# VectorE's list reordered around the copies of the maxima, and the transposed x evacuated by ScalarE, in a windowed-attention layer

## The reference

```python
def _arsinh_norm(x, w, b):
    return w * jnp.arcsinh(x) + b
...
nb_k = kk[:, ri, ci].reshape(B, H, W, k * k, num_heads, hd)
nb_v = v[:, ri, ci].reshape(B, H, W, k * k, num_heads, hd)
scores = jnp.einsum('bijnd,bijmnd->bijnm', q, nb_k)
attn = jax.nn.softmax(scores, axis=-1)
out = jnp.einsum('bijnm,bijmnd->bijnd', attn, nb_v).reshape(B, H, W, C)
return out @ proj_w + proj_b
...
h1 = _arsinh_norm(h, n1_w, n1_b)
h = h + _na2d(h1, qkv_w, qkv_b, proj_w, proj_b)
h2 = _arsinh_norm(h, n2_w, n2_b)
ff = jax.nn.gelu(h2 @ mlp_w1 + mlp_b1, approximate=False) @ mlp_w2 + mlp_b2
return h + ff
```

## Time and profile before

| | |
|---|---|
| median of three runs | 4443.3 us |
| the profiled execution's own time | 4440.94 us |
| its span | 4439.1 us |
| mean granted TensorE clock (share of full speed) | 0.992 |
| TensorE matmul busy | 4159.5 us, 94% |
| VectorE busy | 3926.1 us, 88% |
| ScalarE busy | 3631.7 us, 82% |
| GpSimd busy | 3359.0 us, 76% |

### The profile page before, as it was taken

The page is one execution under the profiler, slowest core; times in us unless marked ns, Lnnn a source line. Parts: engine busy times, 40 slices in busy tenths (PEclk is TensorE's granted clock), DMA queues, the critical chain, the costliest instruction groups (busy, mean ns, idle before and its releaser), DMA issues.

```text
span 4439.1 us, 129514 instructions
## 1 busy us (share of the span) xinstructions
PE 4159.5 (94%) x49224; PEld 2857.8 (64%) x49224; DVE 3926.1 (88%) x8225; ACT 3631.7 (82%) x5377; POOL 3359.0 (76%) x4092
## 2 busy tenths in 40 slices
PE   5999999999999999999999999999999999999997
PEld 3666666666666666666666666666666666666664
DVE  6899999989989998998999899899989989999984
ACT  4888888888888888888888888888888888888884
POOL 2777777777777777777777777777777777777775
PEclk8999999999999999999999999999999999999998
DMA  4555555555555555555555555555555555555551
GB/s 120 132 141 139 142 139 143 136 139 141 141 140 140 142 137 139 141 140 141 140 142 137 140 141 139 140 141 141 139 139 144 136 140 140 141 141 138 142 133 50
DMA packets 644105, 607.94 MB, mean 137 GB/s; under 512 B 77070, under 2 KB 639376, under 8 KB 639888
## 3 DMA queue, kind: packets, MB, share of 16 engines
q1 hardware_dynamic: 643488, 599.66, 51.2%
HBM read 206.02 MB, written 135.40 MB: 77 GB/s over the span
## 4 chain that ended last, share of the span: by engine, by line
DVE 42%; PE 18%; POOL 13%; issue 13%; ACT 12%; SPq 1%; DMA 0%; POOLq 0%; DVEq 0%; ACTq 0%
PE ps L381 16%; POOL b_lo L1163 6%; POOL b_hi L1161 6%; DVE ps L841 5%; DVE queries L860 5%; DVE o_norm L874 4%; DVE ln_u L767 4%; DVE ln_u L760 4%; DVE k_nat L815 4%; ACT L1073 4%; DVE ln_u L763 3%; DVE h L802 3%; ACT p_hi L1064 3%; DVE q_nat L808 3%; ACT prob L1063 2%
## 5 line engine op out<-in xcount | busy, mean ns | idle before, releaser
L1146 POOL TENSOR_TENSOR p_lo<-prob,p_hi 100x512 f16<-100x512 f32 x1024 | 1269.7, 1245 | 619.1 <-ACT p_hi L1064 619.1
L1063 ACT ACTIVATE prob<-ps 100x512 f32<-100x512 f32 x1024 | 610.2, 596 | 51.1 <-PE ps L381 49.3
L874 DVE TENSOR_TENSOR o_norm<-ps,recip 64x128 f32<-64x128 f32 x2048 | 590.2, 288 | 49.3
L1172 POOL TENSOR_TENSOR g_lo<-g,g_hi 128x512 f16<-128x512 f32 x512 | 593.8, 1160 | 41.0
L1064 ACT ACTIVATE p_hi<-ps 100x512 f16<-100x512 f32 x1024 | 616.4, 602 | 0.0
L381 PEld LDWEIGHTS ps<-v_win,p_hi 100*128 100x128 f16 x8192 | 476.0, 98 | 204.7 <-issue 66.9
L381 PE MATMUL ps<-w_hi,g_hi 128*128 128x256 f16 x2048 | 561.1, 274 | 0.0
L841 DVE TENSOR_REDUCE ps<-ps 128x8 f32<-128x800 f32 x512 | 509.1, 994 | 58.6 <-PE ps L381 54.2
L381 PE MATMUL ps<-w_lo,g_hi 128*128 128x256 f16 x2048 | 560.9, 274 | 0.0
L381 PE MATMUL ps<-w_hi,g_lo 128*128 128x256 f16 x2048 | 560.8, 274 | 0.0
L381 PE MATMUL ps<-v_win,p_hi 100*128 100x65 f16 x8192 | 515.6, 193 | 27.0 <-POOL p_lo L1146 18.4
(11 more groups left out here) (100 smaller groups left out, 11497.9 us busy)
## 6 DMA issues: line engine op xcount, KB each, us to landing
keys<-k_win SPq DMA_DIRECT2D x1536, 100.0 KB, 2.3
v_win<-v_rows SPq DMA_DIRECT2D x1024, 101.6 KB
queries<-q_nat SPq DMA_DIRECT2D x1536, 64.0 KB
v_rows<-v_nat SPq DMA_DIRECT2D x256, 260.0 KB, 4.3
xin<-in_x_dram SPq DMA_DIRECT2D x128, 512.0 KB, 4.3
out_dram<-y SPq DMA_DIRECT2D x256, 256.0 KB, 3.0
queries<-in_query_mask_dram SPq DMA_DIRECT2D x128, 224.0 KB
keys<-in_mlp_w_dram SPq DMA_DIRECT2D x2, 512.0 KB, 6.5
```

The costliest lines, as they stand in the source:

```text
L874: s = v.tensor_tensor(o_norm[r, c], av[r, :, HD * e:HD * e + HD], recip[c % 2][r].to_broadcast([NQ, PAIRS, HD]), ALU.mult)
L1063: act.activation(prob[b][0:NK], ps[0:NK, B_ST + b, :], ACT.Exp, scale=INV * INV).then_inc(prob_ready, 1)
L1146: pool.tensor_tensor(p_lo[b][0:NK], prob[b][0:NK], p_hi[b][0:NK], ALU.subtract).then_inc(p_lo_ready, 1)
L1172: pool.tensor_tensor(g_lo[:, m, :], g32[:, m, :], g_hi[:, m, :], ALU.subtract).then_inc(g_lo_ready, 1)
```

## The change

Three things. (1) On VectorE, in slots 2 and 3 the instructions `sign2`, `sign1` and `o_low` 0 come ahead of `maximum`, `maximum_high` and `maximum_low` instead of behind them, with `sign1` now ahead of `o_low`; in slots 0, 1 and 2 the instructions `k_low` 1, `q_low` 1 and `sum1` come ahead of the two copies `maxima_to_queries` instead of behind. (2) `x_from_transposes` leaves VectorE for ScalarE, as an activation Copy with a scale; there it stands around `v_high` 0 in slot 1, behind `root2`. (3) On TensorE, `max_rows` of slot 3 goes behind `mlp_in` 2.

```diff
@@ -195,7 +195,8 @@
             sem("pe_" + s) for s in ("x", "q", "k", "v", "proj", "m1", "m2"))
         pe_s, pe_max, pe_st, pe_av, pe_ot = (sem("pe_" + s) for s in ("s", "max", "st", "av", "ot"))
 
-        xT_ready, h_ready, abs1, abs2, sum1, sum2 = (sem("dve_" + s) for s in ("xT", "h", "abs1", "abs2", "sum1", "sum2"))
+        h_ready, abs1, abs2, sum1, sum2 = (sem("dve_" + s) for s in ("h", "abs1", "abs2", "sum1", "sum2"))
+        xT_ready = sem("act_xT")
         asinh1, asinh2, y_ready = (sem("dve_" + s) for s in ("asinh1", "asinh2", "y"))
         q_lo_ready, k_lo_ready, v_lo_ready, o_lo_ready = (sem("dve_" + s) for s in ("q_lo", "k_lo", "v_lo", "o_lo"))
         max32_ready, max_hi_ready, max_ready, maxima_placed = (
@@ -668,7 +669,7 @@
 
                     if att:
                         weighted(t, par, 2 * k)
-                    if more:
+                    if k < 3 and more:
                         max_rows(ahead[0], ahead[2])
 
                     if k == 0 and post:
@@ -688,6 +689,9 @@
                         turn(t, 0)
                     if k == 3 and post:
                         mlp_in(t - 1, 2)
+                    if k == 3 and more:
+                        max_rows(ahead[0], ahead[2])
+                    if k == 3 and post:
                         mlp_in(t - 1, 3)
 
                     if att:
@@ -751,11 +755,6 @@
                 assert count[0] == V_ALL, count[0]
                 v.memset(keys[:, :, HEADS * TILES * NK:KROW], 0.0).then_inc(keys_zeroed, 1)
 
-            def x_from_transposes(t, u, g):
-
-                v.wait_ge(pe_x, signals(t, G, g + 1))
-                v.tensor_scalar(xT[u][:, g, :], ps[:, X_BANK[g], :], WS, None, ALU.mult).then_inc(xT_ready, 1)
-
             def magnitude(out, of, s):
                 v.tensor_single_scalar(out.bitcast(U32), of.bitcast(U32), MAGNITUDE, ALU.bitwise_and).then_inc(s, 1)
 
@@ -877,8 +876,6 @@
 
             def opening(t):
 
-                x_from_transposes(t + 3, t + 3, 0)
-                x_from_transposes(t + 3, t + 3, 1)
                 if t == -3:
                     magnitude1(0, 0)
                     for t_ in k_win:
@@ -912,6 +909,12 @@
                 for k in range(SLOTS):
                     ta, ka = (t, k + 1) if k + 1 < SLOTS else (t + 1, 0)
                     more = has(ta)
+                    if k == 2 and post:
+                        sign2(t - 1, old)
+                    if k == 3 and fill:
+                        sign1(t + 3, (u + 3) % XT)
+                    if k == 3 and att:
+                        o_low(t, par, 0)
                     if more:
                         maximum(ta, ka)
                         maximum_high(ta, ka)
@@ -923,35 +926,26 @@
                         k_low(t + 2, 0)
                     if k == 1 and pre:
                         q_low(t + 2, par, 0)
-                    if k == 2 and post:
-                        sign2(t - 1, old)
-                    if k == 3 and att:
-                        o_low(t, par, 0)
-                    if k == 3 and fill:
-                        sign1(t + 3, (u + 3) % XT)
 
                     if att:
                         sum_reciprocal(t, 2 * k)
                         normalise(t, 2 * k)
+                    if k == 0 and pre:
+                        k_low(t + 2, 1)
+                    if k == 1 and pre:
+                        q_low(t + 2, par, 1)
+                    if k == 2 and fill:
+                        sum1_(t + 3)
                     if more:
                         maxima_to_queries(ta, par if ta == t else old, ka)
 
-                    if k == 0 and pre:
-                        k_low(t + 2, 1)
                     if k == 0 and post:
                         h_from_projection(t - 1, old, (u - 1) % XT, 0)
                         h_from_projection(t - 1, old, (u - 1) % XT, 1)
-                    if k == 1 and pre:
-                        q_low(t + 2, par, 1)
-                    if k == 1 and fill:
-                        x_from_transposes(t + 3, (u + 3) % XT, 0)
-                        x_from_transposes(t + 3, (u + 3) % XT, 1)
                     if k == 1 and post:
                         sum2_(t - 1)
                     if k == 1 and pre:
                         v_low(t + 2, 0)
-                    if k == 2 and fill:
-                        sum1_(t + 3)
                     if k == 2 and fin:
                         result(t - 2, 0)
 
@@ -992,6 +986,11 @@
 
                 act.wait_ge(ln, signals(t, 1, 1))
                 act.activation(s, s, ACT.Exp, scale=0.5).then_inc(rt, 1)
+
+            def x_from_transposes(t, u, g):
+
+                act.wait_ge(pe_x, signals(t, G, g + 1))
+                act.activation(xT[u][:, g, :], ps[:, X_BANK[g], :], ACT.Copy, scale=WS).then_inc(xT_ready, 1)
 
             def square1(t, u):
                 act.wait_ge(xT_ready, signals(t, G, G))
@@ -1074,6 +1073,8 @@
 
             def opening(t):
 
+                x_from_transposes(t + 3, t + 3, 0)
+                x_from_transposes(t + 3, t + 3, 1)
                 square1(t + 3, t + 3)
                 log_of_square(ln1_s[:], sq1, ln1a, t + 3)
                 root(ln1_s[:], ln1a, root1, t + 3)
@@ -1121,8 +1122,13 @@
                     if k == 1 and post:
                         log_of_square(ln2_s[:], sq2, ln2a, t - 1)
                         root(ln2_s[:], ln2a, root2, t - 1)
+                    if k == 1 and fill:
+                        x_from_transposes(t + 3, (u + 3) % XT, 0)
                     if k == 1 and pre:
                         v_high(t + 2, 0)
+                    if k == 1 and fill:
+                        x_from_transposes(t + 3, (u + 3) % XT, 1)
+                    if k == 1 and pre:
                         v_high(t + 2, 1)
                     if k == 2 and fill:
                         square1(t + 3, (u + 3) % XT)
```

## The result

The changed kernel takes 4766.8 us (4764.67 to 4766.91), the kernel before beside it 4442.4: ratio 1.0729 [1.0708, 1.0750]. Forecast were 4521 and a range that ended at 4540. The sign was right; the loss is 324 us in place of 78. A fourth run of the changed kernel took 5836.72 us at a mean granted clock of 0.656, and is left out as a slow run. The profiled execution takes 4766.82 us, its span is 4765.0.

What follows compares the result with a forecast made beforehand. A ring through all engines, 33.74 us a band, was taken as the bound. Both collisions add 0.63 a band: 123 x 0.63 = 77.5 on 4440.9 gives 4518, with 2.4 to the median 4521; range 4388 to 4540.

Steps and rivals of the forecast that it cites:

- the forecast's case: Slot 0: `magnitude2` stands behind one GpSimd `p_low`, held 0.76 in the replay; band 34.37 with all other steps.
- Ring and span: A ring through all engines sets the 33.74 us band; 0.63 lost per band, times 123, ends left at 0.
- Slot 0, the timing: `k_low` 1 ahead of the copies: `p_low` 2 starts at 13.8, `magnitude2` arrives at 14.01, in its middle.
- Slot 0, the price: Hold of `magnitude2` behind `p_low` 2, bounds 0 and 0.8; 0.8 taken, 0.76 in the replay.
- Slot 1: `q_low` 1 ahead of the copies, x copied by ScalarE: second `x_transposes` 19.10, before 19.25; `v_product` 1 19.69, before 19.84.
- just hidden: Slot 1: ScalarE's copy of x, 18.61 to 19.2, fits behind the transposes (0.59), so `v_product` 1 doesn't wait.
- rival (d): ScalarE, 1.2 us a band fuller, becomes the bound before `v_product` 1: 0 to 0.4 a band; no separate chance given.
- Slot 2: `maximum` waits behind `sign2`, so TensorE's `max_rows` comes 0.62 later; with `mlp_in` 0's wait given back, net 0.28 late.
- Slot 3: `p_low` 6 is first by 0.08, holds `sign1` for 1.0; `mlp_in` 2 starts at 35.10 against 34.43.
- (a): One of two collisions doesn't happen: band 33.99 (about 4474) if `magnitude` isn't held, 34.12 (4490) if `sign1` is first; chance 0.20.
- (c): VectorE never stands behind GpSimd, the four `sum` and `sign` at 1.22 each: band 33.29, 4388; chance 0.27.
- the replay: One band followed from the table load at 4.34 to the next, keeping measured spacings: 38.71 against 38.08.

Runs made afterwards that it cites:

- e2: Changed kernel with one wait added: GpSimd starts `p_low` 2 only after `magnitude2`; 4478.5 us, 1.0084 of the kernel before.
- e6: Changed kernel with one wait added between `p_low` 2 and 3: GpSimd starts `p_low` 3 only after `magnitude2`; 4551.6 us, 1.0253 of the kernel before.
- e3: Kernel before with one edit alone: `k_low` 1 ahead of the copies of the maxima in slot 0; 4550.1 us, 1.0251.
- e7: e2 with three repeats of `magnitude2`'s own operation ahead of it on VectorE, about 1.75 us of plain work intended; 4807.8 us, 1.0832 of the kernel before.
- e1: Changed kernel with one edit undone: `k_low` 1 behind the copies of the maxima again in slot 0; 4571.5 us, 1.0293 of the kernel before.
- e10: e6 with one more wait: GpSimd starts `p_low` 6 only after `sign1`; 4567.4 us, 1.0279 of the kernel before.
- e4: Kernel before with one edit alone: x's two copies out of PSUM on ScalarE, around `v_high` 0; 4455.3 us, 1.0032.
- e8: Kernel before with `q_low` 1 ahead of the copies, x on ScalarE (first copy ahead of `root2`), and last `g_lo` waiting for `sum2`; 4433.5 us, 0.9988.
- e5: Kernel before with only `sign2`, `sign1`, `o_low` 0 ahead of the maxima in slots 2 and 3, and `max_rows` behind `mlp_in` 2; 4586.9 us, 1.0334.

## Why the prediction was right or wrong

The band, step by step of measured kernels, from 33.73:

| | band, us | what is added |
|---|---|---|
| e2 | 34.02 | all edits, `magnitude2` not held |
| e6 | 34.63 | `magnitude2` held by one `p_low` (the forecast's case, 34.37) |
| changed, clock up | 35.60 | held by two |
| changed, clock falls | 36.79 | TensorE at 1.2 GHz behind the stall |

- **Ring and span: right.** The loss is in the band alone, times 123, and a hold of VectorE goes into the band about one for one: a hold of 0.63 costs 0.76 in e3, and 0.61 from e2 to e6.
- **Slot 0, the timing: right.** `k_low` 1 early, ScalarE's windows early, `p_low` 2 ahead of `magnitude2` by 0.39, forecast 0.21. `magnitude2` is held in 125 of 128 bands. The measured hold also settles what no row of before showed: a `magnitude` is held behind GpSimd like `sign`. The Trainium skill ("SBUF — State Buffer", section "Who interferes with whom") says that whoever issues first keeps the shared ports for its whole instruction and the other fully blocks. By that rule the hold ends with `p_low` 2. The trace agrees on the block and shows more: 1.75, past the end of that one instruction.
- **Slot 0, the price: wrong, and this is the first failing step.** "0 (it isn't held) and 0.8 (held like `sign`)" bounded the hold by the rest of one `p_low`. The row that I had in hand says "x2" and 2.43: two instructions without a gap. Both passed: +0.97 a band over e6, 119 us. By the same replay the upper bound should have been the rest of that whole run, 13.8 + 2.43 - 14.01 - 0.13 = 2.1, and the range with it. ("0.13 both times" is by the rows 0.15 and 0.14; that changes nothing.)
- **The clock: not in the sum, the second failure.** Behind the 1.88 stall it falls in two bands of three. Mean band 36.36 against 35.60: 0.76 a band, 93 us. I had said nothing of it, since before has 0.992 throughout; e7 shows that the stall needn't come from the collision, e3 that a single such stall need not bring the fall.
- **Slot 1: right in its rows, wrong in one reason.** `x_transposes` 1 no longer waits; ScalarE's copy takes 0.60. The stall itself, at `max_rows` of slot 1, is in no sentence of the prediction. And that VectorE "reaches `sum_reciprocal` of tile 3 early and waits for TensorE" is not so: in e6, and in the changed kernel's bands without a fall, it has no idle time there. That the copy is "just hidden" depends on slot 0, as e1 shows with 0.97 of waiting. So rival (d), a fuller ScalarE, is real where ScalarE isn't early.
- **Slot 2: right in kind, 0.3 too small.** TensorE waits for the maxima behind `sign2`: 0.7 forecast, 0.52 and 0.88 in the changed kernel, 0.53 in e2, 1.03 in e6, the forecast's case. `mlp_in` 0's wait for b_lo is given back.
- **Slot 3: right in its rows, its worth open.** `sign1` 1.83 and 2.19 (forecast 2.2), `mlp_in` 2 waits 0.33. What undoing it is worth could not be had by itself (e10).
- **The rivals.** (a), "`magnitude` not held", is e2: 33.99 forecast, 34.02 measured, with a wait of 0.40 for `p_low` 2 that the rival didn't have, so the closeness is in part luck. (c), all instructions unheld, is seen nowhere: each edit that freed VectorE moved a held instruction to another place (e4, e8).

Of 246 us between forecast and result, 119 is the second `p_low`, 93 the clock and about 32 the replay's own shortfall (0.26 a band), which arises in slot 2 as e6 shows. Open: why `p_low` 3 gets ahead of a waiting `magnitude2` in the changed kernel and mostly not in e3. The readiness of its input fits band by band, but no run changed it alone. Open too: why one band in three keeps its clock behind the same 1.88 stall, and all nine of e3 do.

## What to carry to other kernels

When an edit makes one engine's instruction arrive earlier, look at what it now meets on the engine with which it shares something, and price the meeting by the whole run of back-to-back instructions there, not by one. Where the meeting can't be avoided, a wait that makes the one with slack yield can be cheap (e2: 288 us for one wait), but only if it has slack (e10). And where every band has a stall of near 2 us on TensorE, the estimate needs a second price, for the clock behind it (here 93 us); the single ones of e3 had none.

## What the runs showed of the hardware

- A waiting `magnitude` (TENSOR_SCALAR, 0.69 by itself) can be passed by a second GpSimd instruction: 2.42 to 2.45 behind two `p_low` in 124 of 128 bands, against 1.32 where it gets in between (116 of 128 in e3) or where the second is made to wait (e6). In e3 the bands part by when the second has its input: 0.37 to 0.50 after the arrival of `magnitude` where it passes, 0.49 to 0.52 where it doesn't.
- Of TensorE's stalls of 1.88, two in three are followed by 1.2 GHz (0.53, 0.50, then 0.97 of full speed in three successive stretches of 1.7 us from 2235.80), of those of 2.25 three in four (e7); each fall costs 1.2 us. No fall is seen behind stalls of 0.97 (e1), 1.03 (e6) and 1.06 (e5), and none behind nine of 1.76 to 1.87 in e3, which stand alone among bands without one.
